# First chunk of a pairwise-interaction kernel in two halves, and an order of all work written as a table

## What is computed

```python
e = jnp.stack([tbl_0[ids[:, 0]], ..., tbl_31[ids[:, 31]]], axis=1)     # 2048 x 32 x 64
row_idx, col_idx = np.triu_indices(32, k=1)                             # 496 pairs of fields
z = jnp.einsum('bpe,fpe,bpf->bp', e[:, row_idx], kernel, e[:, col_idx]) # kernel: 64 x 496 x 64
h = jnp.concatenate([z, dense_ctx], axis=1)                             # 2048 x 512
h = jnp.maximum(h @ W_top1 + b_top1, 0.0)                               # 512
h = jnp.maximum(h @ W_top2 + b_top2, 0.0)                               # 256
y = h @ W_top3
```

## Time and profile before

| | us |
|---|---|
| median of the runs | 830.16 |
| the profiled execution | 830.1 |
| its span, first to last instruction | 827.9 |
| TensorE busy | 765.6 (92%) |
| VectorE busy | 653.6 (79%) |
| ScalarE busy | 626.6 (76%) |
| GpSimd busy | 484.0 (58%) |

### The profile page before, as it was taken

One profiled execution on the slowest core, in us unless ns is written; L12 is line 12 of the kernel. 1 busy time (PEld: TensorE's weight loads), 2 busy tenths in 40 slices (PEclk: granted clock), 3 DMA queues, 4 the chain that ended last, 5 costly groups with the idle time before them and its releaser, 6 DMA issues.

```text
span 827.9 us, 14456 instructions
## 1 busy us (share of the span) xinstructions
PE 765.6 (92%) x3776; PEld 274.8 (33%) x3776; DVE 653.6 (79%) x580; ACT 626.6 (76%) x5033; POOL 484.0 (58%) x518
## 2 busy tenths in 40 slices
PE   0456799999989999999999999999999999999998
PEld 0122233333333333333433333333433333333333
DVE  0246799998869888889878888889878888888950
ACT  0019899876426789899886789899876899999942
POOL 6777777777777777777347777777147772000000
PEclk9988999999999999999999999999999999999999
DMA  9621212111322211121112211121012120010000
GB/s 332 201 51 28 53 27 53 27 29 28 54 53 51 53 28 29 33 48 28 15 40 54 44 35 28 32 49 27 8 39 53 27 54 10 2 27 2 1 1 0
DMA packets 33354, 36.26 MB, mean 44 GB/s; under 512 B 18420, under 2 KB 18676, under 8 KB 33144
## 3 DMA queue, kind: packets, MB, share of 16 engines
q0 software_dynamic: 16384, 16.81, 10.5%
q1 hardware_dynamic: 16888, 18.53, 7.7%
HBM read 26.91 MB, written 0.01 MB: 33 GB/s over the span
## 4 chain that ended last, share of the span: by engine, by line
PE 69%; POOL 12%; issue 10%; DVE 7%; ACT 1%; DMA 1%; DVEq 0%
PE y_ps L447 21%; PE y_ps L460 17%; PE sum_ps L474 13%; POOL rows L352 8%; PE layer_ps L490 6%; DVE products L667 5%; POOL kept_rows L352 4%; PE layer_ps L493 3%; PE y_ps L415 2%; PE y_ps L450 1%; DVE batch_products L678 1%; ACT batch_products L596 1%; PE y_ps L507 1%; DMA rows<-tbl_dram,idx 1%; DVE z_batch L640 1%
## 5 line engine op out<-in xcount | busy, mean ns | idle before, releaser
L596 ACT ACTIVATE batch_products<-batch_products 128x64 f32<-128x64 f32 x2496 | 596.4, 241 | 95.1 <-DVE batch_products L678 95.0
L596 ACT ACTIVATION_READ_ACCUMULATOR batch_products<-batch_products 128x1 f32 x2496 | 468.5, 188 | 0.0
L352 POOL DMA_INDIRECT rows<-tbl_dram,idx x384 | 362.4, 944 | 164.6 <-issue 112.7
L667 DVE TENSOR_TENSOR products<-y_ps,xt 128x1024 f32<-128x1024 f32 x288 | 333.4, 1216 | 81.9 <-PE y_ps L448 81.8
L447 PE MATMUL y_ps<-xt,kernel_sb 64*128 64x512 f32 x576 | 277.0, 617 | 11.4 <-DVE xt L684 9.3
L448 PE MATMUL y_ps<-xt,kernel_sb 64*128 64x512 f32 x576 | 277.1, 617 | 0.0
L678 DVE TENSOR_TENSOR batch_products<-y_ps,kept_rows 128x1024 f32<-128x1024 f32 x192 | 224.1, 1216 | 8.8 <-PE y_ps L462 4.1
L460 PE MATMUL y_ps<-kernel_sb,xt 64*128 64x512 f32 x384 | 190.9, 619 | 3.8 <-DVE products L667 2.8
L462 PE MATMUL y_ps<-kernel_sb,xt 64*128 64x512 f32 x384 | 190.9, 619 | 0.0
L447 PEld LDWEIGHTS y_ps<-xt,kernel_sb 64*128 64x128 f32 x576 | 102.0, 189 | 179.2 <-issue 112.3
L474 PE MATMUL sum_ps<-products,selector 128*32 128x512 f32 x1216 | 150.1, 604 | 1.8 <-DVE products L667 1.4
(11 more groups left out here) (49 smaller groups left out, 279.4 us busy)
## 6 DMA issues: line engine op xcount, KB each, us to landing
special<-xt SPq DMA_DIRECT2D x64, 128.0 KB
kernel_sb<-pair_kernel_dram SPq DMA_DIRECT2D x15, 512.0 KB, 11.2
rows<-tbl_dram,idx POOLq DMA_INDIRECT x384, 2.4
kept_rows<-tbl_dram,idx POOLq DMA_INDIRECT x128, 2.4
w_sb<-w_dram SPq DMA_DIRECT2D x1, 1024.0 KB
w_sb<-w_dram SPq DMA_DIRECT2D x1, 512.0 KB
kernel_sb<-pair_kernel_dram SPq DMA_DIRECT2D x1, 256.0 KB, 3.0
z_batch<-dense_dram SPq DMA_DIRECT2D x16, 8.0 KB
```

Source lines behind the costliest of these rows:

```text
L352: pool.indirect_dma_start(rows_of(c, q, t)[:, h, :], None, tables[j], bass.IndirectOffsetOnAxis(ap=idx[:, n, j:j + 1], axis=0)).then_inc(k ...
L596: last = nc.scalar.activation(product, product, ACT.Copy, accum_out=batch_sums(unit)[:, column:column + 1])
L667: nc.vector.tensor_tensor(products[:, duos % PRODUCT_RING, :, 0:width(c)], y[:, :, 0:width(c)], by, ALU.mult).then_inc(unit_done, 1)
```

## The change

The four chunks stay, but chunk 0 is now two segments, g = 0 with samples 0 to 255 and g = 1 with samples 256 to 511; chunks 1, 2 and 3 are g = 2, 3 and 4. Each segment is gathered, turned, multiplied and summed by itself. In the halves, a quad whose two duos are both block duos becomes one unit: four matmuls of 256 columns side by side in one `y_ps` pair, and one VectorE product of 1024 elements, whose other operand takes two places of `xt` (68 such units). The quads with a special duo remain two units of 512 elements (16 units). Each half has its own semaphores for landings. The batches, 128 samples each, are the same 192.

The rules for the order are gone. A table of 83 bursts gives for each: units of duos or quads, pairs to turn, layer steps ahead, batches, layer steps behind; a T adds turn_batch. The sums of the burst follow. Which batches VectorE adds up stands in `DVE_SHARE`, one in so many for each segment.

```diff
-CHUNK_TILES = (4, 4, 4, 4)
+SEGMENTS = ((0, 0, 2), (0, 2, 4), (1, 0, 4), (2, 0, 4), (3, 0, 4))
+DVE_SHARE = (7, 4, 5, 6, 5)
+BURSTS = (
+    "05010 11020 22040 31010 01010 30010 42010 40010 32040 40020 34040 40010 61000 24040 32040 42030",
+    "30020 43030 40020 42050 60000 30010 32000 42000 30000 50010 32351T 42440 41140 41001 51200 40000",
...
+def units_of(g, quad):
+    pair = (2 * quad, 2 * quad + 1)
+    if half(g) and all(DUO[a][0] == "block" for a in pair):
+        return [("quad", g, quad)]
+    return [("duo", g, a) for a in pair]
...
+    for burst in bursts:
+        duos, turns, before, fill, behind = map(int, burst[:5])
+        for unit in take(units, duos):
+            steps.append(unit)
+            if unit[0] == "quad" or unit[2] % 2:
+                quads.append((unit[1], unit_duos(unit)[-1] // 2))
+        steps += take(layers, before)
+        turned = take(pairs, turns)
+        batches += [("batch", g, q, t) for g, q in turned if q in BATCH_Q for t in tiles(g)]
...
+        steps += take(batches, fill)
+        steps += take(layers, behind)
+        for g, quad in take(quads, len(quads)):
...
+            steps.append(("sum", g, quad))
...
-DVE_SUMS = {unit for n, unit in enumerate(BATCH) if n % (6 if unit[1] else 4) == 1}
+DVE_SUMS = {unit for n, unit in enumerate(BATCH) if n % DVE_SHARE[unit[1]] == 1}
...
+            for g in range(len(SEGMENTS)):
...
                 for q in range(PAIRS):
...
                     elif q >= KEPT + ROW_RING:
-                        pool.wait_ge(unit_ready, TURN_OF[c, q - ROW_RING] + 1)
+                        pool.wait_ge(unit_ready, TURN_OF[g, q - ROW_RING] + 1)
...
-                        for t in range(CHUNK_TILES[c]):
+                        for t in tiles(g):
...
+            def quad(y, g, number):
+                for a in (2 * number, 2 * number + 1):
+                    d, q, place = PLACE[DUO[a]], DUO[a][2], slice(half_place(a) * (N // 2), half_place(a) * (N // 2) + N // 2)
+                    nc.tensor.matmul(y[:, 0, place], kernel_sb[low, d, :], x_of(g, q)[low, :], start=True, stop=True)
+                    last = nc.tensor.matmul(y[:, 1, place], kernel_sb[high, d, :], x_of(g, q)[high, :], start=True, stop=True)
+                last.then_inc(unit_ready, 1)
...
+                    if kind == "quad":
+                        lower, upper = sorted(slot_of(step[1], DUO[a][1]) for a in duos)
+                        by = xt[:, lower:upper + 1:upper - lower, cols].unsqueeze(1).to_broadcast([P, 2, 2, size])
+                        nc.vector.tensor_tensor(into.rearrange("p b (d n) -> p b d n", d=2),
+                                                y[:].rearrange("p b (d n) -> p b d n", d=2), by, ALU.mult).then_inc(unit_done, 1)
```

More of the change, by code:

```diff
@@ L1 @@
+import itertools
 from contextlib import ExitStack
@@ L173, in work_order, with unit_duos @@
-def work_order():
-    order, layers = first_chunk(), []
-    for c in range(1, CHUNKS):
-        order += later_chunk(c, layers)
-    assert not layers
-    return order
-ORDER = work_order()
-UNIT = [step for step in ORDER if step[0] in ("duo", "batch", "turn", "turn_batch")]
+def units_of(g, quad):
[3 more added lines that the diff above has]
+    return [("duo", g, a) for a in pair]
+def unit_duos(unit):
+    return (unit[2],) if unit[0] == "duo" else (2 * unit[2], 2 * unit[2] + 1)
@@ new lines, in burst_order, with take @@
+def burst_order(bursts):
+    units = [unit for g in range(len(SEGMENTS)) for quad in range(QUADS) for unit in units_of(g, quad)]
+    pairs = [(g, q) for g in range(len(SEGMENTS)) for q in range(PAIRS)]
+    steps, layers, batches, quads, towers = [], [], [], [], 0
+    def take(queue, count):
+        assert count <= len(queue)
+        taken = queue[:count]
+        del queue[:count]
+        return taken
+    for burst in bursts:
[7 more added lines that the diff above has]
+        batches += [("batch", g, q, t) for g, q in turned if q in BATCH_Q for t in tiles(g)]
+        while turned:
+            g, q = turned[0]
+            count = 2 if turned[1:2] == [(g, q + 1)] and (chunk(g) * PAIRS + q + 1) % XT_RING else 1
+            steps.append(("turn", g, tuple(q for _, q in take(turned, count))))
+        if burst[5:]:
+            steps.append(("turn_batch", towers))
+            towers += 1
+        steps += take(batches, fill)
+        steps += take(layers, behind)
+        for g, quad in take(quads, len(quads)):
+            if quad == (Z_BANKS - 1) * Z_QUADS:
+                steps.append(("mix", g))
+            steps.append(("sum", g, quad))
+            if quad == QUADS - 1 and g == last_of(chunk(g)) and chunk(g) < CHUNKS - 1:
+                layers += [("layer", chunk(g)) + piece for piece in LAYERS]
+    assert not (units or pairs or batches or layers or quads) and towers == CHUNKS
+    return steps
@@ L553, in _ @@
                 if kind == "duo":
-                    duo(y, step[1], step[2])
+                    duo(y, *step[1:])
+                elif kind == "quad":
+                    quad(y, *step[1:])
                 elif kind == "batch":
@@ L618, in _ @@
                 del open_sums[:len(ready)]
-                if kind in ("duo", "batch", "turn", "turn_batch"):
+                if kind in ("duo", "quad", "batch", "turn", "turn_batch"):
                     g += 1
@@ L637, in sum_batch @@
                 dve.wait_ge(unit_done, UNIT_OF[unit] + 1)
-                if unit[1] and unit[2] < BATCH_Q[MIXED]:
+                if chunk(unit[1]) and unit[2] < BATCH_Q[MIXED]:
                     dve.wait_ge(mixed, unit[1])
```

371 lines of the change are left out of this document (166 added, 205 removed), and 4 rows, old and new, of the table BURSTS.

## The result

| | before | after |
|---|---|---|
| median, us | 830.14 (829.94 to 830.24) | 800.71 (799.88 to 801.31) |
| profiled execution | 830.1 | 800.1 |
| its span | 827.9 | 798.4 |
| TensorE busy | 765.6 (92%) | 751.4 (94%) |

The ratio is 0.9645, 95% interval 0.9628 to 0.9662.

A forecast was written before the change was run, and what follows sets the result against it. Before, gather 224's landing, then TensorE's list, was taken to bound; after, gather 192's. Turn 246.5 + list 532.9 + tail 24.8 = 804.2 span, plus 2.2 around it, 806.4, said as 806.5; range 803 to 815.

The forecast's parts named there:

- The gate's turn: TensorE's turn of pairs 6 and 7 of chunk 1, awaiting gather 192 (243.9 us); forecast at 246.5 us.
- the loss ahead of the gate: Before the turn of pairs 6 and 7, TensorE and VectorE at equal load lose 3.3%, 6.4 us on 193.
- GpSimd has a wait too: Gathers of pair 15, second half, wait for the turn of pairs 11 and 12, moving later gathers 1 to 2 us.
- The ledger: TensorE's list priced by passes and changes of kind; 545.2 us against 544.8 measured from 283.1 to the end in before.
- The list behind: TensorE's work from the turn of pairs 6 and 7 of chunk 1 to the last tower: 532.9 us.
- the floor: Lowest time for the whole kernel, with nothing lost before gather 192 lands: 803.8 us, said as 803.
- a change of kind costs 0.19 more: In TensorE's list, each switch between kinds of work costs 0.19 us; 241 changes behind the turn, 45.8 us.
- Around the span: Time of the execution outside the profiled span, taken from the kernel before: 2.2 us.
- (1): Before the turn of pairs 6 and 7, pace slips further and GpSimd's wait carries it on: 813 to 815; chance 0.15.
- (2): TensorE's list after the turn of pairs 6 and 7 has no reserve and stalls, +3 to 8: 810 to 814; chance 0.13.
- (3): In the first chunk, 256-column passes do not halve; slower from 0.30 us a pass, up to 889; chance 0.05.
- (4): TensorE runs at 1.2 GHz up to chunk 1, 146 us of list double: some 930 us; chance 0.02.

The follow-up runs named there:

- The clocked changed kernel: The changed kernel with every gather replaced by five GpSimd memsets of the same 1.248 us pace, embedding rows left out; 800.11 us, ratio 0.964 to the kernel before.

## Why the prediction was wrong, step by step

**The mechanism held.** Landing of gather 192 plus list behind it sets the end (landings 9.9 us later: 9.9 more), the halves pay only with the order and the order brings only half without the halves, and the 256-wide pass takes half of the 512-wide one. The forecast gain was 23.7 us, the measured one 29.4; the miss is in three terms, all to one side.

**The gate's turn, 246.5 forecast, 244.2 measured: 2.3.** The step that failed is the loss ahead of the gate: "two engines at equal load lose something to each other", priced at 3.3%, and behind it "GpSimd has a wait too". The ledger had TensorE there at 237.0, and it came at 241.3: 4.3 lost on 193, bank ends included, where the prediction gave 8.4. It took the turn of pairs 11 and 12 of the second half at 153.9, the ledger's 154.3, ahead of the 157.8 at which gather 125 was due. So GpSimd did not wait, and the landing stayed within 0.3 us of where it was before. The 3.3% of one stretch of the old order did not carry over to the new. And it was counted twice, once in TensorE and once, through the late turn, in GpSimd.

**The list behind, 532.9 forecast, 529.4 measured (244.2 to 773.6): 3.5.** This is the term that broke the floor. The step that failed is "a change of kind costs 0.19 more", one price for all, in a ledger held to be "right to 0.5 us". Rows of TensorE around the last turn after:

```profile
688.64 0.59 PE L516 MATMUL layer_ps<-z_sb,w_sb 128*128 128x512 f32 x1
689.07 0.60 PE L431 MATMUL y_ps<-identity,rows 128*128 128x128 f32 x4
689.60 0.69 PE L486 MATMUL y_ps<-kernel_sb,xt 64*128 64x512 f32 x1
...
690.14 0.59 PE L486 MATMUL y_ps<-kernel_sb,xt 64*128 64x512 f32 x1
```

The turn starts 0.43 behind the last layer pass, which is that pass and nothing more. The batch starts 0.53 behind the turn, whose four transposes take 0.44, and its second pass 0.54 behind its first in place of 0.43. Two changes make 0.09 + 0.11 = 0.20, not 0.38. Over both traces a fit by kind, an estimate, gives: between units and layer steps 0.20 each way, unit to sum 0.20 but sum to unit 0.13, and 0.20 for both changes around a turn behind a layer step. By these prices the list of before is 517.4, and 520.0 were measured; the trace has 2.1 us of waits of TensorE in that list, which is most of the difference. The flat 0.19 was too dear by about as much as those waits, and the sum came out right; the prediction's "so no other engine costs anything there" did not follow from it. The list of after has more turn steps, 29 for 19, where the flat price errs most: 527.9 by kind, 529.4 measured, 532.9 forecast. A sum that agrees to 0.5 on one order had two errors of 2 to 3 in it; that it agreed was luck, and the forecast's floor rested on that 0.5. A third error is small: six passes in a row take 2.57 us in the kernel before (230.71 to 233.28), 0.429 each and not 0.43, which makes about 1 us over the whole list. These prices hold only where an engine does not wait for another: the moved layer steps should have saved 6 by them and cost 11.4.

**Around the span, 2.2 forecast, 1.7 measured** (800.1 less 798.4). No trace shows what lies there.

2.3, 3.5 and 0.5 make 6.3; 806.4 less 6.3 is 800.1, the profiled execution. Against the sum of the floor, 803.8, the gate is 0.3 later, the list 3.5 shorter and the rest 0.5 shorter.

**The rivals.** (1) and (2) did not come: TensorE waited 2.3 for the landing, and from there to the last tower its waits in the trace are 0.3. But (2) was near. "There is no reserve" is what the moved layer steps show, 11.4 lost to a change that moves 23 of 78 layer steps and adds no work. (3) and (4) have no row for them.

The Trainium skill's page "TensorE: Matmul & The Clock Gate" (Why this matters for your kernels) advises, for products thinner than 512, to pad them or to do all steps of a product before the next transfer, or else the clock swings at every step. The prediction took from it a rule on width alone, which the second half of the advice, on transfers, does not bear out. As a rule on width it does not hold here: the profile after has the clock at 1.00 from 43.0 on, through two halves of 256-wide passes. The clocked changed kernel has 0.75 in a stretch of the same widths, behind a longer wait; so here it is not the width.

**What stays open.** The 1.5 us by which the list of after is longer than its prices by kind, of which the trace shows 0.3 as waits. How the 14 us that the new order saves by itself divide between waits and changes of kind. Why the other engines stand beside real gathers in some groups of runs. And why, there, a whole first chunk with the new order is 2.1 to 2.5% faster than the kernel before, and the full change is not.

## What to carry to other kernels

When landings arrive at a fixed pace, the end is the landing plus what stands behind it. Look for work that can be put ahead of the landing, and then ask whether the engine can have done it by then: here the order found the work and the halves made it possible; the order alone brought half, the halves alone nothing. A ledger that fits one order to 0.5 us may hold two errors that cancel, so fit each price from its own rows and count the waits apart before carrying it to another order. And a step that looks like a costly interruption may be the time in which the next engine catches up; taking it away can cost twice what it seemed to cost.

## What the runs showed of the hardware

Gathers by indirect DMA can come with long stands of the other engines. In some groups of runs VectorE stood for up to 61 us at a time while GpSimd issued them, ScalarE for up to 22 us and TensorE between the passes of one sum; the kernel before took 1292 us in place of 830, and the same engines ran at full pace behind the last gather (109.3 us for the last stretch, as ever). In another group the same kernel took 830.23, with the same gathers. The record gives the same chip number for a group with 1294 and for the one with 830.23, so it is not the chip alone. Five memsets in a gather's place, in SBUF too, never did it: 811, 799, 811 and 806 us in a group in which before took 1277.

The Trainium skill's page "SBUF — State Buffer" (Who interferes with whom) knows one contention among engines, a port pair in SBUF that VectorE and GpSimd share, and says that TensorE and ScalarE wait for nobody. That pair can't be the whole cause of the rows above: TensorE's passes of one sum stand 2.8 us apart too. What does it was not found.

A kernel whose DMAs trouble the measurement can still be studied if another engine's idle time can play their part: the clock of memsets gave 830.45 and 800.11 for 830.14 and 800.71.
